# Second attention's context and mask work cut into smaller pieces, batch by batch, and the ternary weights moved last and onto VectorE

## What is computed

```python
scores = jnp.einsum('bhtd,bhsd->bhts', q, k) / scale
scores = jnp.where(mask, scores, -jnp.inf)
attn = jnp.nan_to_num(jax.nn.softmax(scores, axis=-1), nan=0.0)
out = jnp.einsum('bhts,bhsd->bhtd', attn, v)
...
scale = jnp.mean(jnp.abs(w)) + EPS
q = jnp.clip(jnp.round(w / scale), -1.0, 1.0) * scale
hidden = jax.nn.silu(up) * gate
```

## Time and profile before

| | us |
|---|---|
| median of 3 runs | 1666.31 (1665.42 to 1667.62) |
| profiled execution, its own time | 1664.57 |
| its span | 1663.3 |
| TensorE matmuls busy | 1459.2 |
| VectorE busy | 1226.7 |
| ScalarE busy | 1108.0 |
| GpSimd busy | 795.7 |

### The profile page before, as it was taken

How to read it: one execution, slowest core, us unless ns; L and a number is a source line. 1 busy time by engine, 2 the same in 40 slices (tenths; PEclk the granted TensorE clock), 3 DMA queues, 4 the chain that set the end, 5 groups by cost and what they waited for, 6 DMA issues and landing times.

```text
span 1663.3 us, 25453 instructions
## 1 busy us (share of the span) xinstructions
PE 1459.2 (88%) x8460; PEld 712.2 (43%) x8460; DVE 1226.7 (74%) x2207; ACT 1108.0 (67%) x2020; POOL 795.7 (48%) x626
## 2 busy tenths in 40 slices
PE   5788988888888898788898989899899999999979
PEld 4243343343333353334443534344444455445445
DVE  6666777766785357478887678899588996888937
ACT  4657657756755655476786588677477885888724
POOL 4024023023130001277867669778386876677823
PEclk8798899997989998799999999999999999999989
DMA  4001101201240100100001000000000000000000
GB/s 156 1 21 29 34 1 25 38 1 19 49 172 2 52 1 16 30 20 6 1 1 40 21 21 6 26 1 4 2 27 1 26 1 1 0 1 1 1 0 26
DMA packets 20488, 36.69 MB, mean 22 GB/s; under 512 B 4898, under 2 KB 15238, under 8 KB 19334
## 3 DMA queue, kind: packets, MB, share of 16 engines
q1 hardware_dynamic: 20358, 35.07, 7.3%
HBM read 26.53 MB, written 1.15 MB: 17 GB/s over the span
## 4 chain that ended last, share of the span: by engine, by line
PE 35%; POOL 9%; issue 7%; DVE 5%; ACT 3%; POOLq 0%; DMA 0%; ACTq 0%; DVEq 0%; SPq 0%
PE BK L680 35%; POOL arena L2008 6%; DVE arena L1630 3%; DVE arena L1613 1%; ACT arena L1881 1%; ACT arena L1889 1%; POOL arena L2005 1%; POOL arena L1983 1%; ACT arena L1874 1%; POOL arena L2014 1%; POOL arena L1993 1%; DVE arena L1013 0%; PE BK L993 0%; DVE arena L1644 0%; ACT L1874 0%
## 5 line engine op out<-in xcount | busy, mean ns | idle before, releaser
L680 PE MATMUL BK<-arena 128*128 128x512 bf16 (+14 forms) x8130 | 1413.5, 376 | 170.9 <-DVE arena L1451 37.0
L680 PEld LDWEIGHTS BK<-arena 128*128 128x128 bf16 (+7 forms) x8130 | 674.9, 115 | 879.4 <-issue 219.6
L2008 POOL TENSOR_TENSOR arena<-arena 128x512 f32<-128x512 f32 (+1 forms) x352 | 509.5, 1447 | 178.3 <-ACT arena L1874 154.3
L1630 DVE TENSOR_TENSOR arena<-arena 128x512 bf16<-128x512 f32 (+1 forms) x416 | 512.5, 1241 | 41.8 <-ACT arena L1881 41.1
L1874 ACT ACTIVATE arena<-BK,arena 128x512 f32<-128x512 f32 (+1 forms) x416 | 286.5, 689 | 131.1 <-PE BK L680 117.4
L1780 ACT ACTIVATE arena<-BK 128x512 f32<-128x512 f32 (+1 forms) x416 | 227.3, 604 | 88.8 <-PE BK L680 83.2
L1451 DVE TENSOR_REDUCE arena<-BK 128x1 f32<-128x512 f32 x384 | 244.3, 684 | 57.0 <-PE BK L680 56.0
L1881 ACT CAST arena<-arena 128x512 bf16<-128x512 f32 (+1 forms) x416 | 253.9, 610 | 0.0
L1889 ACT ACTIVATE arena<-BK 128x512 bf16<-128x512 f32 (+1 forms) x256 | 130.2, 509 | 87.0 <-PE BK L680 86.9
L1613 DVE CUSTOM_DVE_ANT_0 arena<-BK,arena 128x512 bf16<-128x512 f32 (+1 forms) x256 | 145.7, 569 | 44.7 <-PE BK L680 38.8
L1927 POOL TENSOR_TENSOR arena<-arena 128x256 f32<-128x256 f32 (+6 forms) x45 | 30.2, 672 | 184.1 <-ACT arena L1717 181.7
(11 more groups left out here) (175 smaller groups left out, 842.0 us busy)
## 6 DMA issues: line engine op xcount, KB each, us to landing
arena<-arena SPq DMA_DIRECT2D x144, 50.0 KB, 2.2
arena<-in_ctxT SPq DMA_DIRECT2D x8, 800.5 KB, 4.3
arena<-in_ctxk SPq DMA_DIRECT2D x4, 768.0 KB
arena<-in_wo SPq DMA_DIRECT2D x1, 2048.0 KB, 7.6
arena<-in_wqT SPq DMA_DIRECT2D x1, 2048.0 KB, 7.7
arena<-in_x SPq DMA_DIRECT2D x4, 256.0 KB, 9.8
arena<-in_rsel SPq DMA_DIRECT2D x1, 1024.0 KB, 9.5
arena<-in_rw1T SPq DMA_DIRECT2D x1, 1024.0 KB, 5.1
```

The costliest lines, as they stand in the source:

```text
L680: return T.matmul(out_, lhsT, rhs, start=start, stop=stop, skip_group_check=True)
L1630: V.tensor_tensor(Pl[k][0:m, :], P1[k][0:m, :], Ph[k][0:m, :], ALU.subtract).then_inc(p_low, 1)
L2008: G.tensor_tensor(acc[0:m, g % 2, :], acc[0:m, g % 2, :], P1[k][0:m, :], ALU.add).then_inc(summed1, 1)
```

## The change

Contexts: `cx` and `cy` are cut in halves (801 and 800 columns; 673 and 672), VectorE's step becomes pieces of its own, `cz`, one or more background slots behind `cx`. Masks: three pieces become seven; halves of L1011, halves of L1013, the middle piece (one more short instruction), halves of L1026; GpSimd's part stays in the last piece, in four instructions. Ternary: quarters of 512 columns, a comparison into `low_` and one instruction that compares and subtracts, both on VectorE. The background is advanced at tiles 1, 3, 6, 9 and 11, batch by batch, held until tile 104 and tile 208, and all ternary work comes last. In stage 1 batch 0's context and mask take eight steps instead of six.

```diff
         def context():
-            piece("cx", 0)
-            yield
-            yield
-            piece("cy", 0)
+            piece("cx", 0, 0)
+            piece("cx", 0, 1)
+            yield
+            piece("cz", 0, 0)
+            yield
+            piece("cz", 0, 1)
+            piece("cy", 0, 0)
             piece("mbl")
             yield
-            for k in range(3):
-                piece("mk", 0, k)
-                yield
+            piece("cy", 0, 1)
+            piece("mk", 0, 0)
+            yield
+            piece("mk", 0, 1)
+            piece("mk", 0, 2)
+            yield
+            piece("mk", 0, 3)
+            piece("mk", 0, 4)
+            yield
+            piece("mk", 0, 5)
+            yield
+            piece("mk", 0, 6)
+            yield
...
         def masked(b):
...
-            for k in range(3):
+            for k in range(7):
                 piece("mk", b, k)
                 yield
 
         def context(b):
             piece("cxl", b)
             yield
-            piece("cx", b)
-            yield
-            piece("cy", b)
-            yield
+            yield
+            for kind in ("cx", "cz", "cy"):
+                for half in range(2):
+                    piece(kind, b, half)
+                    yield
...
-                for c in range(2):
+                for c in range(4):
                     piece("twd", i, c)
                     yield
                     piece("twe", i, c)
...
-        bg = chain(context(1), values(1), masked(1), self.norm(to, 2, 2), self.norm(to, 2, 3), context(2), values(2),
-                   context(3), values(3), masked(2), ternary(0), masked(3), ternary(1, 2))
+        now = [0]
+
+        def later(tile):
+            while now[0] < tile:
+                yield
+
+        bg = chain(context(1), values(1), masked(1), self.norm(to, 2, 2),
+                   later(104), self.norm(to, 2, 3), context(2), values(2), masked(2),
+                   later(208), context(3), values(3), masked(3), ternary(0, 1, 2))
...
-            if kt % 4 == 1:
+            if kt in (1, 3, 6, 9, 11):
                 next(bg, None)
...
+            own = ((0, HALF), (HALF, S2))
+            if k < 2:
...
+                V.tensor_tensor_reduce(out=kept[:, w_], in0=cth[:, b, w_], in1=mb8[:, w_], scale=1.0, scalar=0.0,
+                                       op0=ALU.mult, op1=ALU.add,
+                                       accum_out=mst[:, k:k + 1]).then_inc(dve_chain.sem, dve_chain.up())
+            elif k < 4:
+                V.tensor_reduce(mst[:, k:k + 1], mb8[:, slice(*own[k - 2])], AX.X,
+                                ALU.add).then_inc(dve_chain.sem, dve_chain.up())
+            elif k == 4:
                 V.tensor_scalar(off, mb8[:, :], 1.0, None, ALU.subtract).then_inc(mask_done, 1)
...
+                V.tensor_tensor(mst[:, 4:6], mst[:, 0:4:2], mst[:, 1:4:2], ALU.add).then_inc(dve_chain.sem, dve_chain.up())
...
             else:
+                w_ = slice(*own[k - 5])
...
+                t = V.scalar_tensor_tensor(out=kept[:, w_], in0=off[:, w_], scalar=mst[:, 0:1], in1=kept[:, w_],
+                                           op0=ALU.mult, op1=ALU.add)
...
                 elif kind == "twd":
                     k, c = arg
-                    w_ = slice(1024 * c, 1024 * c + 1024)
+                    w_ = slice(512 * c, 512 * c + 512)
...
-                    V.tensor_scalar(qa[:, :], wr[:, w_], hs_[:, k, 0:1], None, ALU.is_gt).then_inc(t_gt, 1)
+                    V.tensor_scalar(low_[:, :], wr[:, w_], hs_[:, k, 1:2], None, ALU.is_lt).then_inc(t_lt, 1)
                 elif kind == "twe":
                     k, c = arg
...
-                    V.tensor_scalar(qb_[:, :], wr[:, w_], hs_[:, k, 1:2], None, ALU.is_lt).then_inc(t_gt, 1)
+                    w_ = slice(512 * c, 512 * c + 512)
+                    dve.wait_ge(t_lt, 4 * k + c + 1)
+                    V.scalar_tensor_tensor(out=tw[k][:, w_], in0=wr[:, w_], scalar=hs_[:, k, 0:1], in1=low_[:, :],
+                                           op0=ALU.is_gt, op1=ALU.subtract).then_inc(tern_done, 1)
...
                 elif kind == "cxl":
                     b, = arg
                     sp.wait_ge(ct_done, 2 * b)
-                    sp.wait_ge(mx_ready, min(b, 2))
+                    sp.wait_ge(mx_ready, b)
...
                 elif kind == "twl":
                     k, = arg
-                    sp.wait_ge(tern_done, 2 * k)
-                    sp.wait_ge(mx_ready, 4 if k else 3)
+                    sp.wait_ge(tern_done, 4 * k)
+                    sp.wait_ge(mx_ready, 4)
```

More of the change, by code:

```diff
@@ L543, in stage2 @@
             g, kt = s // NKT, s % NKT
+            now[0] = s
             while g < NG and g not in rowed:
@@ L814, in program @@
         ckf = sb("ckf", [128, NKT, 128], F32, L1)
-        qa, qb_ = (arena[:, (L1.at - 6656) // 4 + 512 * i:(L1.at - 6656) // 4 + 512 * i + 512].bitcast(BF16) for i in range(2))
+        low_ = arena[:, (L1.at - 6656) // 4:(L1.at - 6656) // 4 + 256].bitcast(BF16)
         mrw = sb("mrw", [128, 2, 512], BF16, SM)
@@ new lines, in dve_mask @@
+            if k < 2:
+                w_ = slice(*own[k])
+                if k == 0:
+                    dve.wait_ge(ld_row, 16 * (b + 1))
+                    dve.wait_ge(*emptied("fold", H - 1))
+                    dve.wait_ge(ct_high, 2 * b + 2)
+                    dve.wait_ge(mx_ready, b)
+                    if b:
+                        dve.wait_ge(ct_done, 2 * b + 2)
+                V.tensor_tensor_reduce(out=kept[:, w_], in0=cth[:, b, w_], in1=mb8[:, w_], scale=1.0, scalar=0.0,
[5 more added lines that the diff above has]
+            elif k == 4:
@@ L1020, in dve_mask @@
                 dve.wait_ge(dve_chain.sem, dve_chain.n)
-                V.scalar_tensor_tensor(out=mst[:, 4:5], in0=mst[:, 0:1], scalar=-1.0, in1=mst[:, 3:4], op0=ALU.mult,
+                V.reciprocal(mst[:, 7:8], mst[:, 6:7]).then_inc(dve_chain.sem, dve_chain.up())
+                dve.wait_ge(dve_chain.sem, dve_chain.n)
+                V.scalar_tensor_tensor(out=mst[:, 0:1], in0=mst[:, 4:5], scalar=-1.0, in1=mst[:, 7:8], op0=ALU.mult,
                                        op1=ALU.mult).then_inc(dve_chain.sem, dve_chain.up())
@@ L1029, in pool_mask @@
+                if k == 6:
+                    t.then_inc(mk_done, 1)
         def pool_mask(b, k):
-            if k == 2:
+            if k == 6:
                 kept, _ = mask_temp(b)
@@ L1046, in program @@
                              "diag_done", "ck_high", "ck_low", "tern_done"))
-        l1_set, t_gt, t_half, dn_recip, pv_taken = (sem(n) for n in ("l1_set", "t_gt", "t_half", "dn_recip", "pv_taken"))
+        l1_set, t_lt, t_half, dn_recip, pv_taken = (sem(n) for n in ("l1_set", "t_lt", "t_half", "dn_recip", "pv_taken"))
         def prep_over(queue):
@@ L1973, in gpsimd_main @@
                     G.tensor_tensor(hsh[:, ch, :], hsh[:, ch, :], sr[:, :], ALU.mult).then_inc(hs_done, 1)
-                elif kind == "cx":
-                    b, = arg
-                    pool.wait_ge(ct_high, b + 1)
+                elif kind == "cx" and arg[1]:
+                    b = arg[0]
+                    pool.wait_ge(ct_high, 2 * b + 1)
                     pool.wait_ge(*filled("fold", H - 1))
@@ L1979, in gpsimd_main @@
                 elif kind == "cy":
-                    b, = arg
-                    pool.wait_ge(ct_step_high, b + 1)
-                    for lo, hi in ((0, 448), (448, 896), (896, S2 - 256)):
+                    b, half = arg
+                    pool.wait_ge(ct_step_high, 2 * b + half + 1)
+                    for lo, hi in (((0, 337), (337, 673)), ((673, 1009), (1009, S2 - 256)))[half]:
                         t = G.tensor_tensor(ctl[:, b, 256 + lo:256 + hi], ctf[b][:, lo:hi], dch[b][:, lo:hi], ALU.subtract)
-                    t.then_inc(ct_done, 1)
+                    if half:
+                        t.then_inc(ct_done, 1)
                 elif kind == "mk":
```

52 lines of the change are left out of this document (19 added, 33 removed).

## The result

The changed kernel takes 1653.01 us (median of 5 runs, 1650.59 to 1655.34), the kernel before in the same rounds 1666.31 (1660.09 to 1670.06): a ratio of 0.9911, 95% interval 0.9888 to 0.9935. It is faster, but by some 13 us, where I forecast 37, and 1653 lies above the range of 1610 to 1650. The profiled execution took 1650.62 us.

A forecast was written before the change was run, and what follows sets the result against it. It took TensorE's idling and lost clock behind side work on VectorE as the cost above a 24.25 us group floor. Gains 14 + 14 + 7 + 2.6 - 0.8, about 37 us, gave 1629 us, range 1610 to 1650.

The forecast's parts named there:

- The floor and the sign: Loop groups without side work take 24.25 us each, TensorE nearly always busy; the change was given 0.93 to be faster.
- My signs of no wait over 2 us and of 1.00 from group 1 on: In the loop, outside output projections, no TensorE wait over 2 us; granted clock at 1.00 from group 1 on.
- before's 56 us: Loop groups with side work: excess over the floor from contexts with values 20.75, masks 26.0 and ternary 9.5 us.
- the price of a late VectorE: VectorE side pieces in the loop: those of 0.9 to 1.3 us were taken to cost 0.5 us each.
- My bound from above: VectorE side pieces in the loop: a piece of 0.9 to 1.3 us costs at most its own length.
- The term of 2.4: Ternary part: new pieces and a late load cost 2.4 us in place of 9.5, 7 us gained.
- late load: First ternary load needs the last mask piece, so the first `twa` comes 1.2 us late.
- Masks and contexts: Side work in the loop: cut masks cost 12 us instead of 26, cut contexts 6.5 instead of 20.75; 14 gained each.
- The moved norm: Batch 3's norm falls in group 8, its transposes between two output projections: 0.8 us more.
- Before the loop: Ahead of the loop, batch 0's mask in halves over more steps: 2.6 us gained, bounds 0 to 5.
- Banks: Rival for the maxima's banks: pieces at tiles 1, 9 and 11 cost full length, 1643 us; chance 0.19.
- Bound: Rival for VectorE: each small piece also costs a GpSimd addition ahead of it, slower at 1675 us; chance 0.05.

The follow-up runs named there:

- thin additions: The changed kernel with GpSimd's additions (all but the first of each group) over 64 of 512 columns: loop 817.8 us, 1597.36 us in one run.
- The thin kernel of before: The kernel before the change with GpSimd's additions (all but the first of each group) over 64 of 512 columns: loop 841.8 us, 1614.21 us in one run.

## Why the prediction was wrong

**The floor and the sign** held. Clean groups take 24.25 us, cutting the side work up helps, and TensorE's waits of over 4 us are gone from the loop, with all but 6.8 us of the low clock. My signs of no wait over 2 us and of 1.00 from group 1 on both failed, by 3.16 and 2.40 us and in groups 2 and 25. Most of the 15.3 us came from the clock, which stood inside before's 56 us and had no term of its own in my sum; TensorE's waits, which the pieces were to shorten, fell by 5.4 us.

**The step that failed** is the price of a late VectorE: "pieces of 0.9 to 1.3 us cost between 0 and their own length; I take 0.5 us each". It was a flat price, by length, at any tile. Measured, the same piece costs from nothing to 2.0 us, more than its own length, and which of these is settled by what GpSimd is doing when it starts and by the tile. In all, side work that I had at 21.7 us took 41. My bound from above was wrong for that reason: it left out the second meeting, that of the remainder behind the piece. Group 23 had shown it (0.74 and 1.42 for the same comparison), and I read it as a matter of size.

**`twe`** is the clearest case. I chose 0.69 us and a cost of 0.05, as for `twa`, since L1026 had never stretched beside GpSimd. Its shortest is 0.736, but it is not `twa`'s kind: `twa` (one input) stays at 0.670 to 0.686 in all 12 cases, while `twd` and `twe` run to 1.50 and 1.42. The term of 2.4 measured 12.2; it is 1.4 when the tiles are chosen. L1026's steadiness was four cases, 1.88 us long each; its halves range from 1.024 to 1.959, so four equal durations were too few to lean on. The term of 2.4 also holds the late load, which came as forecast.

By the Trainium skill ("SBUF — State Buffer", "Who interferes with whom") a VectorE instruction with two SBUF inputs, or in a mode that uses both ports, which its one-input `tensor_scalar` can enter, and a GpSimd instruction that reads SBUF block each other whole, and a `tensor_reduce` on this chip never does. The traces agree in all three: L1716 and L1711 stretch, L1692 does not, and with thin additions both medians fall to 0.747 and 0.482. "Whole" is a little too strong for these rows: the blocked `twe` of group 21 ends 0.54 us after the addition it met, less than its shortest 0.736. I had cited half of this rule as speaking against `twe` and then priced by a row instead.

**Masks and contexts**, forecast at 12 and 6.5 and a gain of 14 each, gave 6.5 and 7.2 when undone alone. The middle step with its four short ones, 1.6 us in my sum, is 1.1 us for L1043, 1.23 for L1045 and more behind it, since L1045, with two inputs, waits for an addition however small it is. In the contexts I had 1.2 us a batch, 3.6 in all, for ScalarE's and GpSimd's pieces with the values; the waits for L2056 alone, nearly all behind `cy` and the values on tiles 1 and 3, are 7.9. Over the whole loops they are 9.6, where before had 8.2: cutting these pieces did not shorten them.

**The moved norm** fits: group 8 is 3.6 us over 40.6, and with my share of 2.8 for the first norm instructions, which no run takes apart, 0.8 remains. What I had missed stands further on, the 2.40 us of group 25, where a ternary piece meets a norm.

**The late load** was right: the first `twa` waited 1.32 us for it, where I had 1.2. A timeline row of after:

```profile
1265.92 0.69 DVE L1692 TENSOR_REDUCE arena<-arena 128x1 f32<-128x512 f32 x1 [1.32 <-DMA arena<-in_wup]
```

**Before the loop** no gain can be seen. TensorE still waits for VectorE behind batch 0's mask, 2.23 us where it had been 2.63:

```profile
651.64 0.60 PE L702 MATMUL BK<-arena 128*128 128x512 bf16 x2 [2.23 <-DVE arena L1614]
```

The stretch ahead of the loop took 701.1 us in after's profile and 698.8 in before's, inside its spread from run to run, so my 2.6 can be neither seen nor excluded.

**The rivals.** "Banks" (1643) had the nearest time: excess with waits until the maxima at pieces at tiles 9 and 11. It priced these at their full length, and they cost up to that plus a second meeting. "Bound" had the right mechanism, a GpSimd addition met by each piece, and the wrong extent: it charges every piece at every tile. Its count of 24 mask pieces should be 21, seven in each of three batches, so that it would decide from 1.10 us a piece on, not 1.04. None of the rivals tied the price to the tile and the kind of instruction at once. In total: 37 forecast, less about 10 for the ternary pieces, 9 for masks and contexts, 2.6 ahead of the loop, is about 15, and the loop gave 15.3.

## What to carry to other kernels

A piece of side work has no price of its own. It is the wait for the GpSimd instruction running when it starts, if it is of a kind that shares with GpSimd, plus what the next shared instruction then waits, and it is paid only at tiles where someone needs VectorE soon. So sort pieces by that kind and by engine first and give each sort its own tiles (14.6 us here with the same instructions), and cut them second (15.3 with the new order). Take the time at half clock apart from the waits before pricing either; and when a row of before is stretched in some cases and not in others, ask what ran beside it before taking the median as its length.

## What the runs showed of the hardware that I had not expected

- Size is no protection: an addition of two numbers a partition (L1045) takes 1.226 us in the median with GpSimd adding 512 columns beside it, 0.270 with 64 columns and 0.151 at its shortest.
- VectorE and GpSimd take turns in these rows. After a stretched piece GpSimd's next addition starts first again, and the second VectorE instruction waits as well: 1.42 and then 1.75 us in group 21, 1.68 and 1.74 in group 18.
- The remainder of 512 columns, with thin additions, has a median of 0.693 us against 1.180: 0.49 of its 1.18 us in the median is waiting. The thin kernel of before, its line L1630, has the same (1.206 in the earlier trace rows):

```profile
L1630 DVE TENSOR_TENSOR arena<-arena x416: 669/692/2187, 697.9 to 1539.7; 128x512 bf16<-128x512 f32 x128, 65x512 bf16<-65x512 f32 x11
```

- The same wait of TensorE (2.40 and 2.39 us, group 25) was followed by 3.4 us at 1.2 GHz in one profile and by none in the next; those 3.4 us cost 1.7.
- The loop repeats to within 2 us, while the 700 us ahead of it spread over 11 us. They are at 1.2 GHz for 119.1 to 150.2 us; the three shortest (694.7 to 696.7) have 119.1 to 120.5, the longest (705.9) has 150.2, but between them the order is not the same. What sets that was not tried.
